# Attention after three LoRA layers on one Trainium2 core: factors stored by head and group, the second normalisation between the root's steps, and other places for the next weights

## The chip, the cores and the metric

The kernel runs on one core of a Trainium2 chip. The time is the device time of one execution in microseconds (us). The engines are called PE (the matmul engine), DVE (VectorE), ACT (ScalarE), POOL (GpSimd) and SP (the queue that issues most loads). PEld is PE's loading of the stationary operand, which runs beside the matmul before it.

## The reference

Four residual layers: a gated MLP with low-rank additions, two linear layers with low-rank additions, and attention over a paged cache. The change touches only the attention:

```
x = x + L3(x)          # x: 8 samples x 128 tokens x 512
q = rope(rmsnorm(x Wq^T)); k = rope(rmsnorm(x Wk^T)); v = x Wv^T    # 32 query heads, 8 key heads, D = 128
k_all = [cached keys (512), k]; v_all = [cached values (512), v]      # 640 keys per sample
scores = q k_all^T / sqrt(D);  cached keys past the length masked with -1e30
probs = softmax(scores);  o = probs v_all;  L3 = o Wo^T
```

## The kernel before

The first 290 us are the three low-rank layers. Then follows the attention in 32 units: 4 pairs of key heads (`NPAIR`), and for each pair the 8 samples. A unit has 8 query heads in two groups of 4 (`G` = 2, `REP` = 4). Every product runs in three passes of split operands (high x high, high x low, low x high), so each operand has a high part (a rounding copy, made by ACT) and a low part (the difference, made by DVE, or by POOL for weights, cached keys and values).

The program is written as turns. Each engine has its own function `turn`, and the order within it is the order of its queue; nothing is reordered by a scheduler. A turn does the front of unit n (projections, norms, rotation, scores, masks, exponentials) and the back of unit n-1 (transposes of the probabilities, sums over values, normalisation, output multiplication), interleaved by hand. There are 33 turns: the first has a front only, the last a back only, and 31 have both.

PE in a turn with both halves: transposes of the first group's probabilities, projection of the second four query heads, values of group 0 and of group 1 (`sums`, L1432), the output multiplication of the first four heads (12 matmuls, L1512), four transposes of rotated queries (L1416), six output matmuls, two transposes of rotated keys, six output matmuls, four transposes of the second queries, then eight scores of six matmuls (L1462) with the next unit's 24 projection matmuls (L1395) between them. Both sets of query transposes use `bank1`, and the second must wait until ACT has made the high part (`high`, L1575) and DVE the low part (`low`, L1746) of the first. The first query transposes wait for `s_rope`, which DVE raises after it has multiplied the new keys by the root.

DVE: copy of the queries, the reciprocal of the softmax denominators (`shares`, L1765), low parts of group 0's probabilities (L1732, L1738), the rotation of the first four queries and the keys (L1721 to L1727), low parts of group 1, the normalisation of group 0 (`normalise`, L1773), the reciprocal square root of the norms by three Newton steps of three small instructions each (`root_end`, L1710 to L1712), two scales from it (L1714, L1715), the keys multiplied by the root (L1808), the normalisation of group 1, the rotation of the second four queries with the low part of group 1's values (L1777) inside it, the low parts for the scores, the mask of the cached keys (L1760), and a mask with maximum for each head (L1753, L1756).

The normalisation multiplies values that lie as [feature, query] by 1/denominator, which DVE has as [query, head]. ACT therefore stores the 128 x 8 reciprocals to DRAM (L1607, after `s_rden`) and loads them back spread over all 128 partitions (L1618, after the store's semaphore `s_den`). DMA issues stand in ACT's queue like its other instructions: what is written behind an issue that waits is not begun.

Weights of the next pair come in 20 chunks of 256 KB: SP loads them into a ring, ACT makes the high part (`high_weights`, L1555), POOL the low part (`low_weights`, L1218). Chunks 0 to 11 are made in the last sample's turn (`extra == "next"`, three times), at places given by the table `EARLY` and by `late`; chunks 12 to 19 in the turn after it (`"out"`). POOL's low parts in a "next" turn begin after the first rotation and after the room for the output is free; chunks 4 and 5 wait for the second rotation (`s_rope`).

## Time and profile before

| | us |
|---|---|
| median of 3 runs | 1467.98 (1465.78 to 1471.86) |
| the profiled execution | 1468.85 |
| its span | 1467.2 |
| PE busy | 1381.8 (94%) |
| DVE busy | 1051.9 (72%) |
| ACT busy | 804.4 (55%) |
| POOL busy | 449.0 (31%) |
| chain that ended last: PE, DVE, issue, ACT, DMA | 70%, 13%, 7%, 6%, 3% |
| DVE's reciprocals of two middle turns start at | 612.71 and 648.26 |
| the same around a turn with next weights | 537.89 and 577.29 |

The page says for each engine how long it was busy, and which chain of work ended last. The share of time by engine is an average over the first 290 us and the attention; the turn-by-turn rows below are of one turn in the middle of the second pair, which repeats with little change, and of one "next" turn. In a row of the timeline the bracket tells how long the engine was idle before it and what ended that.

### The profile page before, as it was taken

How to read it: one execution, taken by the hardware profiler on the slowest of the kernel's cores; microseconds unless marked ns; L12 is line 12 of the kernel's file. 1: busy time of each engine (PE TensorE's matmuls, PEld its weight loads, DVE VectorE, ACT ScalarE, POOL GpSimd, SP SyncE). 2: the span in 40 equal slices, each digit the busy share in tenths (PEclk: the TensorE clock that was granted, in tenths of full speed). 3: DMA queues.
4: the chain of work that ended last, by engine and by line, in shares of the span. 5: the costliest groups of instructions: out<-in, count | busy, mean ns of one | idle time of the engine just before them, and what ended most of it. 6: DMA issues, size and time to landing. Idle time of an engine off the chain costs nothing.

```text
span 1467.2 us, 26375 instructions
## 1 busy us (share of the span) xinstructions
PE 1381.8 (94%) x7308; PEld 1157.6 (79%) x7308; DVE 1051.9 (72%) x2569; ACT 804.4 (55%) x1888; POOL 449.0 (31%) x483
## 2 busy tenths in 40 slices
PE   5999999989999999999999999999998999999996
PEld 5888888878888887888888778877887888888884
DVE  4532447778777787777777777777777777777774
ACT  5532334375555556655555666555556665555553
POOL 4000000562222236522222455222224552222321
PEclk9999999999999999999999999999999999999998
DMA  8111303553333344333232452332225522222211
GB/s 307 45 58 44 108 18 117 198 181 75 81 80 78 74 124 143 90 77 73 72 72 72 136 149 74 73 72 72 72 73 148 138 73 72 75 76 72 72 37 29
DMA packets 149049, 135.59 MB, mean 92 GB/s; under 512 B 95360, under 2 KB 114176, under 8 KB 148736
## 3 DMA queue, kind: packets, MB, share of 16 engines
q1 hardware_dynamic: 127328, 83.35, 20.4%
q0 software_dynamic: 11728, 34.09, 8.2%
q10 hardware_dynamic: 9936, 17.45, 4.4%
q8 instruction: 29, 0.48, 0.1%
q14 instruction: 28, 0.23, 0.0%
HBM read 117.89 MB, written 16.91 MB: 92 GB/s over the span
## 4 chain that ended last, share of the span: by engine, by line
PE 70%; DVE 13%; issue 7%; ACT 6%; DMA 3%; POOL 0%; SPq 0%; DVEq 0%; ACTq 0%; POOLq 0%
PE bank L1395 16%; PE wide L1462 14%; PE tail L1512 7%; PE wide L1427 7%; PE tail L1432 6%; DVE tail L1773 5%; PE wide L423 4%; PE wide L491 3%; ACT oT L1583 3%; ACT prT L1579 2%; DVE oT L1777 2%; PE tail L423 2%; PE bank L423 2%; PE wide L550 2%; DMA spread<-one_over_denominators 2%
## 5 line engine op out<-in xcount | busy, mean ns | idle before, releaser
L1587 ACT ACTIVATE pr<-pr,nm,q_scale 128x640 f32<-128x640 f32 x256 | 236.4, 923 | 91.0 <-DVE nm L1756 89.1
L1753 DVE CUSTOM_DVE_ANT_0 pr<-wide,bias 128x640 f32<-128x640 f32 x256 | 210.0, 820 | 84.9 <-issue 84.8
L1432 PE MATMUL tail<-prT,vt 128*128 128x512 f32 x960 | 262.7, 408 | 4.6 <-DVE prT L1738 2.4
L1512 PE MATMUL tail<-woT,oT 128*128 128x512 f32 x768 | 205.3, 412 | 42.0 <-DVE oT L1777 42.0
L1201 POOL TENSOR_TENSOR tick<-tick 128x1 f32<-128x1 f32 x127 | 26.2, 206 | 614.1 <-PE wide L1462 524.4
L1432 PEld LDWEIGHTS tail<-prT,vt 128*128 128x128 f32 x960 | 168.0, 188 | 54.7 <-DVE prT L1738 17.0
L1512 PEld LDWEIGHTS tail<-woT,oT 128*128 128x128 f32 x768 | 140.2, 192 | 84.6 <-DVE oT L1777 49.4
L1732 DVE TENSOR_TENSOR prT<-wide,prT 128x1024 fp32r<-128x1024 f32 x128 | 153.8, 1222 | 62.0 <-ACT prT L1579 61.8
L1462 PE MATMUL wide<-kT,qT 128*128 128x320 f32 x512 | 161.7, 316 | 0.5 <-DVE mx L1753 0.5
L1462 PE MATMUL wide<-kT_low,qT 128*128 128x320 f32 x512 | 158.7, 310 | 0.0
L1462 PE MATMUL wide<-kT,oT 128*128 128x320 f32 x512 | 158.4, 309 | 0.0
L1579 ACT CAST prT<-wide 128x1024 fp32r<-128x1024 f32 x128 | 126.8, 1016 | 53.3 <-PE wide L1427 52.0
L1583 ACT CAST oT<-tail 128x512 fp32r<-128x512 f32 x64 | 37.5, 587 | 194.5 <-DVE tail L1773 194.5
L1427 PEld LDWEIGHTS wide<-ident,pr 128*128 128x128 f32 x1024 | 115.4, 141 | 20.0 <-issue 9.0
L1427 PE MATMUL wide<-ident,pr 128*128 128x128 f32 x1024 | 128.8, 274 | 0.9 <-DVE mx L1753 0.9
L1395 PE MATMUL bank<-wkvT,xTb 128*128 128x512 f32 x372 | 111.5, 394 | 0.0
L1395 PE MATMUL bank<-wq0T,xTb 128*128 128x512 f32 x372 | 106.2, 393 | 0.0
L1462 PEld LDWEIGHTS wide<-kT,qT 128*128 128x128 f32 x512 | 96.7, 189 | 10.7 <-DVE mx L1753 1.0
L1462 PEld LDWEIGHTS wide<-kT_low,qT 128*128 128x128 f32 x512 | 96.7, 189 | 8.9
L1462 PEld LDWEIGHTS wide<-kT,oT 128*128 128x128 f32 x512 | 96.6, 189 | 0.0
L1240 POOL TENSOR_TENSOR vt<-v_raw,vt 128x1280 fp32r<-128x1280 f32 x32 | 95.1, 2973 | 2.6
L1395 PE MATMUL bank<-wq1T,xTb 128*128 128x512 f32 x372 | 92.9, 398 | 0.0
(236 smaller groups left out, 2555.8 us busy)
## 6 DMA issues: line engine op xcount, KB each, us to landing
w_ring<-pair_weights SPq DMA_DIRECT2D x80, 256.0 KB, 4.2
k_raw<-k_pages SPq DMA_DIRECT2D x512, 32.0 KB, 2.8
v_raw<-v_pages SPq DMA_DIRECT2D x512, 32.0 KB, 1.7
spread<-one_over_denominators ACTq DMA_DIRECT2D x32, 512.0 KB, 4.5
xTb<-x_transposed POOLq DMA_DIRECT2D x31, 512.0 KB, 4.8
out<-y POOLq DMA_DIRECT2D x32, 256.0 KB, 6.0
rope<-rope_tables SPq DMA_DIRECT2D x31, 256.0 KB, 2.6
w_raw<-w_gate_up SPq DMA_DIRECT2D x10, 512.0 KB, 3.3
```

The costliest lines, as they stand in the source:

```text
L423: last = nc.tensor.matmul(gate_up_place(j, c, w), wT[:, j % 2, w, w_part, k, :], x_half(x_part, k, c), start=(k == 0 and w_part + x_part = ...
L1240: nc.gpsimd.tensor_tensor(vt[1][:, :, :], v_raw[:, :, :], vt[0][:, :, :], ALU.subtract).then_inc(s_vs, 1)
L1395: last = nc.tensor.matmul(bank[i][:, :], x[:, x_part, k, :], w[:, w_part, k, :], start=(step == 0), stop=(step == NPROD - 1))
L1427: last = nc.tensor.transpose(wide[w][:, c * P:(c + 1) * P], piece, ident[:, :])
L1432: last = nc.tensor.matmul(tail[g][:, :], vt[v_part][:, j, g * D:(g + 1) * D], prT[p_part][:, j, :], start=(j == 0 and v_part + p_part == 0 ...
L1462: last = nc.tensor.matmul(out, (qT, qT_low)[q_part][:, g, i * S:(i + 1) * S], (kT, kT_low)[k_part][:, g, c * (NK // 2):(c + 1) * (NK // 2) ...
L1512: last = nc.tensor.matmul(tail[0][:, :], oT[:, o_part, h // REP, (h % REP) * S:(h % REP + 1) * S], woT[w_part][:, h, :], start=(h == 0 and ...
L1579: ac.copy(prT[0][:, 2 * w:2 * w + 2, :], wide[w][:, :].rearrange("p (j c) -> p j c", j=2)).then_inc(s_phi, 1)
L1583: ac.copy(oT[:, 0, g, :], tail[g][:, :]).then_inc(s_ohi, 1)
L1587: ac.activation(pr[h][:, :], pr[h][:, :], ACT.Exp, bias=nm[:, h:h + 1], scale=q_scale[:, 0, head(h)], accum_out=den[:, h:h + 1]).then_inc( ...
L1732: v.tensor_tensor(prT[1][:, 2 * w:2 * w + 2, :], wide[w][:, :].rearrange("p (j c) -> p j c", j=2), prT[0][:, 2 * w:2 * w + 2, :], ALU.subt ...
L1753: v.tensor_tensor_reduce(halves(pr[h][:, :]), scores, halves(bias[:, :]), 1.0, -3.0e38, ALU.add, ALU.max, mx[:, h:h + 1]).then_inc(s_sfree, 1)
```

## The change

- The scratch in DRAM for the reciprocals is laid out by group, head and query, where it was by query and head. Each group has its own store and its own spread, with semaphores of their own. The store's runs are single elements; the spread tile is read contiguously by `normalise`, where it was read with a step of 8 elements.
- Group 0's reciprocals are computed at the end of the turn before, ahead of the last mask; its store is the first thing of ACT's back half. The spreads stand behind the first and behind the second squares.
- DVE: the Newton steps are apart, with the second normalisation between the first and the second step and the low part of group 1's values between the second and the third. The two scales stand behind the second rotation. In a "next" turn the root begins behind the low values of group 0.
- PE: the first query transposes wait for the first rotation (`s_step`), no longer for the keys' multiplication; the key transposes wait for that.
- The high parts of the next weights: chunk 0 before the copy of the second queries, chunk 1 before group 1's first high part, chunks 2 and 3 before its second, 4 and 5 behind the values, 6, 7 and 8 between the high parts of queries and keys, 9 to 11 among the exponentials.

The diff, with unchanged stretches cut:

```diff
--- before.py
+++ after.py
...
     rope_scratch = nc.dram_tensor("rope_tables", [B, P, 4 * D], F32).ap()
-    share_scratch = nc.dram_tensor("one_over_denominators", [P * HP], F32).ap()
+    share_scratch = nc.dram_tensor("one_over_denominators", [G, REP * S], F32).ap()
...
     pr = [place(135168 + h * 2560 if h < 6 else 163840 + (h - 6) * 2560, f"pr{h}", [P, NK]) for h in range(HP)]
-    spread = place(135168, "spread", [P, P, HP])
+    spread = place(135168, "spread", [P, G, REP * S])
     k_raw = place(155648, "k_raw", [P, NPP, G, PSIZE])
...
     s_rden = sem("denominator_ready")
-    s_den = sem("one_over_denominators_stored")
-    s_spread = sem("one_over_denominators_spread")
+    s_den = [sem(f"one_over_denominators_stored{g}") for g in range(G)]
+    s_spread = [sem(f"one_over_denominators_spread{g}") for g in range(G)]
     s_norm = sem("values_normalised")
...
     NSTEP = 16
+    TURNED = 2
     TURN = [FRONT[i] + BACK[i] for i in range(2)]
...
-    EARLY = {"next": ((0,), (1,), (2, 3), (4, 5, 6, 7), (8,), (9,), (10,)), "out": ((), (), (), (), (12, 13), (14,), (15,)), None: ((),) * 7}
+    EARLY = {"next": ((0,), (1,), (2, 3), (4, 5), (6,), (7,), (8,)), "out": ((), (), (), (), (12, 13), (14,), (15,)), None: ((),) * 7}
...
         if extra == "next":
-            return [11] if h == 3 else []
+            return [h + 7] if 2 <= h < 5 else []
         return [h + 14] if extra == "out" and 2 <= h < 6 else []
...
-        TURNED, MASKED = 2, NSTEP
+        MASKED = NSTEP
...
-                pe.wait_ge(s_rope, n * G + 1 + FIRST)
+                pe.wait_ge(s_step, n * NSTEP + TURNED)
                 transposes(1, [ra[:, i, :] for i in range(REP)])
...
             if front:
+                pe.wait_ge(s_rope, n * G + 1 + FIRST)
                 transposes(0, [ra[:, REP + i, :] for i in range(G)])
...
+            def early(place):
+                for i in EARLY[extra][place]:
+                    if i == 0:
+                        act.wait_ge(c_full[0], before[0] + 1)
+                        act.wait_ge(c_full[1], before[1] + 1)
+                    high_weights(chunk_pair(pair, extra), i)
+            def store_shares(g):
+                act.wait_ge(s_rden, u * G + g + 1)
+                act.dma_start(share_scratch[g].rearrange("(i p) -> p i", p=P), rden[:, g * REP:(g + 1) * REP],
+                              allow_slow_non_contiguous=True).then_inc(s_den[g], 16)
+            def spread_shares(g):
+                act.wait_ge(s_den[g], u * 16 + 16)
+                act.dma_start(spread[:, g, :], share_scratch[g:g + 1].to_broadcast([P, REP * S])).then_inc(s_spread[g], 16)
...
             if back:
+                store_shares(0)
                 high_probs(0, 0)
-                act.wait_ge(s_rden, u + 1)
-                act.dma_start(share_scratch.rearrange("(p h) -> p h", h=HP), rden[:, :]).then_inc(s_den, 16)
+                store_shares(1)
                 high_probs(0, 1)
...
             if back:
-                act.wait_ge(s_den, u * 16 + 16)
-                act.dma_start(spread[:, :, :].rearrange("p q h -> p (q h)"),
-                              share_scratch.rearrange("(o n) -> o n", o=1).to_broadcast([P, P * HP])).then_inc(s_spread, 16)
+                spread_shares(0)
             if front:
+                early(0)
                 arrive()
...
                     act.wait_ge(s_xs[0], 16 * BLK)
-            def early(place):
-                for i in EARLY[extra][place]:
-                    if i == 0:
-                        act.wait_ge(c_full[0], before[0] + 1)
-                        act.wait_ge(c_full[1], before[1] + 1)
-                    high_weights(chunk_pair(pair, extra), i)
             if back:
-                early(0)
+                spread_shares(1)
+                early(1)
                 high_probs(1, 0)
-                early(1)
+                early(2)
                 high_probs(1, 1)
...
                 copy_values(0)
-            early(2)
             own = BACK[0] if back else 0
...
-            def root_end():
+            def newton():
                 x_, y_, t_ = var[:, :], rs[:, :], nt[:, :]
-                for _ in range(3):
-                    then(v.tensor_tensor(t_, y_, y_, ALU.mult))
-                    then(v.scalar_tensor_tensor(t_, t_, -0.5, x_, ALU.mult, ALU.mult))
-                    then(v.scalar_tensor_tensor(y_, t_, 1.5, y_, ALU.add, ALU.mult))
+                then(v.tensor_tensor(t_, y_, y_, ALU.mult))
+                then(v.scalar_tensor_tensor(t_, t_, -0.5, x_, ALU.mult, ALU.mult))
+                then(v.scalar_tensor_tensor(y_, t_, 1.5, y_, ALU.add, ALU.mult))
+            def scales():
                 v.tensor_scalar(q_scale[:, 0, :], rs[:, :], SCALE, None, ALU.mult)
...
-            def rotate(h0, m0, kinds, between=None):
+            def rotate(h0, m0, kinds):
                 for k0, m, kind in kinds:
...
                     v.tensor_tensor(o, q, cos_w.to_broadcast([P, m, D]), ALU.mult)
-                    if between:
-                        between()
                     v.tensor_tensor(s[:, :, 0:half], q[:, :, half:D], sin_w[:, :, 0:half].to_broadcast([P, m, half]), ALU.mult)
...
-            def shares():
-                dve.wait_ge(s_exp, u * HP + HP)
-                v.reciprocal(rden[:, :], den[:, :]).then_inc(s_rden, 1)
+            def shares(of, g):
+                dve.wait_ge(s_exp, of * HP + (g + 1) * REP)
+                v.reciprocal(rden[:, g * REP:(g + 1) * REP], den[:, g * REP:(g + 1) * REP]).then_inc(s_rden, 1)
...
                 dve.wait_ge(s_pv, u * G + g + 1 + FIRST)
-                if g == 0:
-                    dve.wait_ge(s_spread, u * 16 + 16)
-                summed = tail[g][:, :].rearrange("p (i q) -> p i q", i=REP)
-                v.tensor_tensor(summed, summed, spread[:, :, g * REP:(g + 1) * REP].rearrange("p q i -> p i q"), ALU.mult).then_inc(s_norm, 1)
+                dve.wait_ge(s_spread[g], u * 16 + 16)
+                v.tensor_tensor(tail[g][:, :], tail[g][:, :], spread[:, g, :], ALU.mult).then_inc(s_norm, 1)
...
             if back:
-                shares()
+                shares(u, 1)
                 low_probs(0, 0)
...
                 low_probs(1, 0)
-            if front:
+            if front and extra != "next":
                 root_begin()
...
             if front:
-                root_end()
+                if extra == "next":
+                    root_begin()
+                newton()
+            if back:
+                normalise(1)
+            if front:
+                newton()
+            if back:
+                low_values(1)
+            if front:
+                newton()
                 keys = ra[:, REP:REP + G, :]
                 v.tensor_tensor(keys, keys, rs[:, REP:REP + G].rearrange("p (h o) -> p h o", o=1).to_broadcast([P, G, D]), ALU.mult).then_inc(s_rope, 1)
-            if back:
-                normalise(1)
-                if not front:
-                    low_values(1)
-            if front:
-                rotate(REP + G, REP, ((REP + G, REP, 0),), (lambda: low_values(1)) if back else None).then_inc(s_rope, 1)
+                rotate(REP + G, REP, ((REP + G, REP, 0),)).then_inc(s_rope, 1)
+                scales()
...
                     mask_max(h)
+                    if h == HP - 2:
+                        shares(n, 0)
                 assert at.n == NSTEP, at.n
```

What this moves, from the instructions as they stand in the program. First DVE in the last sample's turn of the first pair, before, from the third Newton step on (`nt`, `rs`: its steps; `q_scale`: the scales; `tail<-tail,spread`: the normalisation; `oT<-tail,oT`: the low part of the values):

```order
L1710 TENSOR_TENSOR nt<-rs 128x10
L1711 SCALAR_TENSOR_TENSOR nt<-nt,var 128x10
L1712 SCALAR_TENSOR_TENSOR rs<-nt,rs 128x10
L1714 TENSOR_SCALAR q_scale<-rs 128x10
L1715 TENSOR_SCALAR q_scale<-rs 128x10
L1808 TENSOR_TENSOR ra<-ra,rs 128x256
L1773 TENSOR_TENSOR tail<-tail,spread 128x512
L1721 TENSOR_TENSOR ra<-qk,rope 128x512
L1777 TENSOR_TENSOR oT<-tail,oT 128x512
L1724 TENSOR_TENSOR rb<-qk,rope 128x4x64
L1725 TENSOR_TENSOR rb<-qk,rope 128x4x64
```

and now, from the second normalisation on:

```order
L1781 TENSOR_TENSOR tail<-tail,spread 128x512
L1721 TENSOR_TENSOR nt<-rs 128x10
L1722 SCALAR_TENSOR_TENSOR nt<-nt,var 128x10
L1723 SCALAR_TENSOR_TENSOR rs<-nt,rs 128x10
L1785 TENSOR_TENSOR oT<-tail,oT 128x512
L1721 TENSOR_TENSOR nt<-rs 128x10
L1722 SCALAR_TENSOR_TENSOR nt<-nt,var 128x10
L1723 SCALAR_TENSOR_TENSOR rs<-nt,rs 128x10
L1826 TENSOR_TENSOR ra<-ra,rs 128x256
L1733 TENSOR_TENSOR ra<-qk,rope 128x512
L1734 TENSOR_TENSOR rb<-qk,rope 128x4x64
L1735 TENSOR_TENSOR rb<-qk,rope 128x4x64
```

The normalisation of group 1 stood behind all steps, the scales and the keys' multiplication (`ra<-ra,rs`). Now two of the three Newton steps and the keys stand behind it, and the scales further down.

Then ACT in the same turn, before, from the spread's issue to the high part of the queries (`wkvT`, `wq0T`: chunks of the next weights; `prT`: high parts of the probabilities, one instruction for half a group, the last for its new keys):

```order
L1618 DMA spread<-one_over_denominators 128x1024
L1622 COPY qk<-bank 128x512
L1569 ACTIVATE bank,ss<-bank 128x128 x4
L1555 CAST wkvT<-w_ring 128x512
L1579 CAST prT<-wide 128x1024
L1555 CAST wkvT<-w_ring 128x512
L1579 CAST prT<-wide 128x1024
L1642 CAST prT<-bank 128x512
L1583 CAST oT<-tail 128x512
L1555 CAST wkvT<-w_ring 128x512 x2
L1583 CAST oT<-tail 128x512
L1555 CAST wq0T<-w_ring 128x512 x4
L1575 CAST qT<-bank 128x512
```

and now:

```order
L1608 DMA spread<-one_over_denominators 128x512
L1557 CAST wkvT<-w_ring 128x512
L1641 COPY qk<-bank 128x512
L1571 ACTIVATE bank,ss<-bank 128x128 x4
L1608 DMA spread<-one_over_denominators 128x512
L1557 CAST wkvT<-w_ring 128x512
L1581 CAST prT<-wide 128x1024
L1557 CAST wkvT<-w_ring 128x512 x2
L1581 CAST prT<-wide 128x1024
L1655 CAST prT<-bank 128x512
L1585 CAST oT<-tail 128x512 x2
L1557 CAST wq0T<-w_ring 128x512 x2
L1577 CAST qT<-bank 128x512
```

Before the high part of the queries (`qT`) stood four chunks behind the second copy of values (`oT`); now two. Chunks 0, 2 and 3 stand earlier.

## Rows read from the trace of the kernel before

**Rows 1.** Waits, whole span: engine line <- releaser: us in total, times, longest
```profile
PEld tail L1512 <- DVE oT L1777: 49.4, 31, 1.9
```

**Rows 2.** Timeline, weight loads, middle turn: start us, us, what, xcount [idle before <-releaser]
```profile
659.17 1.22 PEld L1432 LDWEIGHTS tail<-prT,vt 128*128 128x128 f32 x6 [0.26 <-DVE prT L1732]
...
660.87 0.53 PEld L1432 LDWEIGHTS tail<-prT,vt 128*128 128x128 f32 x3 [0.48 <-DVE prT L1738]
...
661.68 2.61 PEld L1512 LDWEIGHTS tail<-woT,oT 128*128 128x128 f32 x12 [0.29 <-issue]
...
666.45 1.23 PEld L1512 LDWEIGHTS tail<-woT,oT 128*128 128x128 f32 x6 [1.53 <-DVE oT L1777]
...
669.33 0.59 PEld L1416 LDWEIGHTS bank<-ident,ra 128*128 128x128 f32 x4
```

**Rows 3.** Timeline, DVE, the same turn
```profile
659.03 1.19 DVE L1773 TENSOR_TENSOR tail<-tail,spread 128x512 f32<-128x512 f32 x1
...
660.13 0.68 DVE L1738 TENSOR_TENSOR prT<-bank,prT 128x512 fp32r<-128x512 f32 x1
...
660.87 0.69 DVE L1777 TENSOR_TENSOR oT<-tail,oT 128x512 fp32r<-128x512 f32 x1
...
661.48 0.16 DVE L1710 TENSOR_TENSOR nt<-rs 128x10 f32<-128x10 f32 x1
...
663.31 0.17 DVE L1714 TENSOR_SCALAR q_scale<-rs 128x10 f32<-128x10 f32 x1
...
663.59 0.42 DVE L1808 TENSOR_TENSOR ra<-ra,rs 128x256 f32<-128x256 f32 x1
...
663.93 1.12 DVE L1773 TENSOR_TENSOR tail<-tail,spread 128x512 f32<-128x512 f32 x1
...
665.71 0.69 DVE L1777 TENSOR_TENSOR oT<-tail,oT 128x512 fp32r<-128x512 f32 x1
```

**Rows 4.** Timeline, DVE, the first turn, second rotation to the low part
```profile
305.69 0.68 DVE L1721 TENSOR_TENSOR ra<-qk,rope 128x512 f32<-128x512 f32 x1
...
307.69 0.68 DVE L1746 TENSOR_TENSOR oT<-bank,qT 128x512 fp32r<-128x512 f32 x1
```

**Rows 5.** Timeline, ACT and its queue, the middle turn
```profile
648.50 0.33 ACTq L1607 DMA_DIRECT2D one_over_denominators<-rden  x1
...
654.59 1.01 ACT L1579 CAST prT<-wide 128x1024 fp32r<-128x1024 f32 x1 [0.41 <-PE wide L1427]
```

**Rows 6.** DMA issues: out<-in, queue, xcount, KB each, us to landing
```profile
spread<-one_over_denominators ACTq DMA_DIRECT2D x32, 512.0 KB, 4.5
...
one_over_denominators<-rden ACTq DMA_DIRECT2D x32, 4.0 KB, 1.4
...
seqlens<-itok_B SPq DMA_DIRECT2D x1, 4.0 KB, 3.5
...
bias<-L_cond_bias SPq DMA_DIRECT2D x1, 2.0 KB, 4.0
```

**Rows 7.** Timeline, POOL, DVE, PE and ACT, the first turn with next weights
```profile
546.43 2.53 POOL L1218 TENSOR_TENSOR wkvT<-w_ring,wkvT 128x512 fp32r<-128x512 f32 x2
...
546.51 1.23 DVE L1705 TENSOR_SCALAR rs<-var 128x10 int32<-128x10 int32 x1
...
551.53 1.27 DVE L1710 TENSOR_TENSOR nt<-rs 128x10 f32<-128x10 f32 x1
...
556.29 0.66 PE L1416 MATMUL bank<-ident,ra 128*128 128x128 f32 x4 [1.52 <-DVE ra L1808]
...
558.63 2.93 PE L1512 MATMUL tail<-woT,oT 128*128 128x512 f32 x6 [1.68 <-DVE oT L1777]
...
561.59 1.63 PE L1512 MATMUL tail<-woT,oT 128*128 128x512 f32 x6
...
557.75 2.18 ACT L1555 CAST wq0T<-w_ring 128x512 fp32r<-128x512 f32 x4
```

**Rows 8.** Windows, same turn: us, busy (x instructions) by engine, PEclk, DMA share, GB/s
```profile
559.00:562.00 3.00, 3.00 (x10) 2.27 (x10) 1.62 (x3) 2.06 (x5) 1.88 (x2) 0.58 0.25 56
```

## The prediction, made before the changed kernel was run

> **What bounds the kernel now.** I read the chain that ended last first: the matmul engine, PE, holds most of it and DVE comes next. Then the waits: the longest stall of PE that comes back regularly is in front of the output multiplication, 31 times, 49.4 us in total, and always behind the same DVE line [rows 1]. Then one middle turn (a "turn" is one sample of one pair of key heads, about 35.5 us long, 32 of them), engine by engine. On PE's weight loads the reader should see four holes after the scores of the turn are read: 0.26, 0.48, 0.29 and 1.53 us [rows 2]; almost everywhere else the loads are back to back, so a middle turn has about 2.6 us to win and little more. DVE's rows [rows 3] tell why the 1.53 exists: between 661.48 and 663.59 DVE does the whole root (nine small steps and two scales), then multiplies the new keys, and only at 663.93 normalises the second group, 1.12 us long, though PE had delivered it by then. ScalarE's copy and DVE's low part follow, and PE continues at 666.45.
>
> **Second normalisation between the root's steps, and contiguous factors.** The first normalisation starts at 659.03 and the next DVE row stands 1.10 later; the low-part row of equal size (128x512 from PSUM against an SBUF tile) takes 0.68 to 0.69 [rows 3]. The old factors are read with a step of 32 bytes, the new ones contiguously. The trace has no contiguous multiplication that writes PSUM, so I bound it: 1.19 (nothing gained) to 0.69. I take 0.69, the row that differs only in where the result goes.
> Then, in the same turn's clock: first normalisation 659.03 to 659.72; low part of the new keys' probabilities starts at 659.63 instead of 660.13 and is done at 660.31. PE's loads of the block before it end at 659.17 + 1.22 = 660.39, so the 0.48 hole closes. The first group's low part starts 0.50 earlier too, at 660.37, and PE starts the output multiplication at 661.18 instead of 661.68. First root step 660.98 to 661.60 (three ops at 0.205: 661.48 to 663.31 is nine of them). Second normalisation 661.60 to 662.29; PE's last three sums, begun at 660.39, are through by then. The second group's low part followed the start of its normalisation by 1.78 (663.93 to 665.71, with ScalarE's copy between them), now by 1.78 - 0.43 = 1.35: 662.95 to 663.64, and the second root step (0.6) fits in beside the copy. PE's twelve output matmuls take 2.61 [rows 2], to 663.79, and the four query transposes 0.59, to 664.4: the second group is ready 0.7 us before PE asks for it. The 1.53 goes.
>
> **Transposes of queries not held for keys.** They now wait for the rotation, which is over long before. In a middle turn this is worth nothing by itself (PE came at 661.68 + 2.61 = 664.3, the keys were multiplied from 663.59 on), but it is needed: the keys' multiplication moves back to about 664.2 (third root step from 663.56). The two key transposes follow six output matmuls (1.23), at 665.7, when the keys have been ready since 664.6. Nothing lost.
>
> **What is late next.** PE reaches the last four transposes 2.88 after it resumed the output multiplication, as before (666.45 to 669.33 [rows 2]): 664.5 + 2.9 = 667.4. They overwrite the bank whose low part DVE must have read. DVE: rotation from 664.52 (the keys' multiplication takes 0.34 to the next start); with nothing inside it, it takes 2.00 from its first op to the low part (305.69 to 307.69 [rows 4]), plus 0.28 for the two scales, now behind it (663.31 to 663.59 [rows 3]), so the low part starts at 666.80 and ends at 667.48. PE goes on at 667.52. **A middle turn gains 669.33 - 667.52 = 1.81 us.** From there on the order is that of before (eight scores with 24 projection matmuls, PE without holes). The one reciprocal put before the last mask costs 0.2 on DVE, inside the pause that DVE has before each mask, since PE's scores set the pace there. If I am wrong on the contiguous reading, both normalisations are 0.5 longer: the 0.48 hole stays, the DVE chain ends 0.94 later, and the turn gains 0.87.
>
> **Factors by head and group.** Before, one store of 128 runs of 32 bytes, issued at 648.50 [rows 5], landing after 1.4, then one spread of 512 KB, 4.5 [rows 6]. Now two stores, each of 512 runs of 4 bytes, and two spreads of half the size. The first store's factors are computed in the turn before, so it goes out by 648 or earlier. No row shows such a store. The nearest is the bias load, 512 elements of 4 bytes one by one: 4.0 us against 3.5 for its neighbour with 128 runs of 32 bytes [rows 6], so 0.5 for 384 more runs. Bounds for the store: 1.4 (runs are free) to 5.6 (all of the 1.4 grows with the runs, times 4); I take 1.9, by the bias row. Then both stores land by 651; the first spread goes out at about 650.5, the second behind the second squares, by 654.6 at the latest; with the old 4.5 they land at 655.0 and 659.1, and the normalisations ask at 659.0 and 661.6. Covered. The wait to look at is not DVE's but ScalarE's: its issue of the second spread waits for the second store, and the high part of the second group's probabilities (654.59 [rows 5]) is queued behind it; PE waits for that at once. The cover is 654.59 - 648.50, less 0.3 for issuing the spread: about 5.8 us from the store's issue.
> The Trainium skill, DMA: Bandwidth & Descriptors, Rules for kernel authors, speaks against this edit: a non-contiguous last dimension becomes one descriptor per element, and one should rearrange. The bias row agrees that it costs something, 0.5 us, but not that it matters here; should each descriptor cost its full share, the sum is that of the third rival.
>
> **Other places for the next weights.** Three turns carry the next pair's weights. In the one at 538 to 577, PE waits 1.52 before the query transposes and 1.68 before the output multiplication, and the six matmuls after that take 2.93 where the next six take 1.63 [rows 7]; the granted clock is 0.58 over 559 to 562 [rows 8], so after these two waits PE was for a while at the lower of its two levels. Two things made it late: DVE's small root steps stretched from 0.17 to 1.2 when GpSimd was subtracting weights (1.23 at 546.51, beside GpSimd's two from 546.43 to 548.96; 1.27 at 551.53), and ScalarE had four weight chunks (2.18) ahead of the queries' high part. After: chunks 2 and 3 go before the second high part, where ScalarE waits for PE; GpSimd's four subtractions, 1.27 each from 546.43, end near 551.5, and the root begins near 551.0 (0.5 ahead of 551.53), so about 0.5 of collision is left. Gain: 1.52 + 1.68 + 1.30 = 4.5, and the 0.5 further up cancels the collision's. **4.5 us in each of three turns.** Bounds: 1.8 (as a middle turn) to 6.
>
> **The sum**, against the profiled execution (1468.85 us; the median of the runs shown is 1467.98, 0.9 less). 31 turns have both halves: 28 x 1.81 = 50.7; 3 x 4.5 = 13.5; the last half turn 0.5 by the shorter first normalisation; the first turn nothing, since its low part still gates it. Together 64.7: 1404.2, and 1403.3 against the median. I say 1404.
>
> **The rivals.**
> *A: the strided read was not the cost.* The multiplications stay at 1.15, since both results go to PSUM, which no other DVE row shows. For it: that absence. Against: 0.46 more than each row of equal size. 28 x 0.87 + 3 x 3.5 = 35: 1433.
> *B: the weight turns gain no more than the others*, because the second rotation's signal, which lets GpSimd start the next subtractions, now stands ahead of the two scales; or because the store, with 4 times the runs, meets the weight loads in the queues. For it: a root step held for 1.23 beside GpSimd. Against: each scale takes 0.17 and stands right behind the signal, so both may have begun before GpSimd does. 31 x 1.81 + 0.5 = 57, less 1.3 in six turns = 49: 1419.
> By the Trainium skill, SBUF — State Buffer, Who interferes with whom, a DVE op in its two-port mode and a GpSimd op exclude each other for the whole instruction; the stretched root steps agree with that.
> *C, on the other side: the 4-byte store holds ScalarE.* If a store takes 5.6 and the second queues behind the first, it lands near 648 + 11.2 = 659, ScalarE's high part comes some 4.5 late, and each turn loses 4.5 - 1.8 = 2.7: 31 x 2.7 = 84, 1552. It decides from about 5.8 us after the issue; the gain is eaten at 5.8 + 1.8 = 7.6. Against it: the bias row, and that 1.4 is mostly the same for any size.
>
> **How the numbers follow.** Forecast 0.67, A 0.12, B 0.13, C 0.08, of which 0.06 slower, 0.01 no change. A measurement of this kernel can tell about 0.5% (7 us). So faster 0.93, same 0.01, slower 0.06. The range: below, if all holes but 0.26 and 0.29 close and the weight turns give 6: 28 x 2.0 + 18 + 0.5 = 75, 1393; above it takes in A, 1436. What is left out is C and a little more.
>
> **What would show it.** The hole of 1.53 before the output multiplication gone; DVE's two normalisations at about 0.69; a wait of 0.1 to 0.2 before the last four transposes, released by DVE's low part of the queries; turn period 33.7 between two reciprocals of the same group; weight turns under 36; ScalarE's second spread issued near 653, without holding the high part behind it; store landing near 2. Wrong if the normalisations stay at 1.15, or the second spread goes out after the high part's place.

## The result, and the profile after

The changed kernel takes 1625.8 us (median), the kernel before 1467.4: ratio 1.106 (95% interval 1.102 to 1.111), 158 us slower. One of its four runs took 1838.4 at a granted clock of 0.726; the ratio is of the other three (1621.3 to 1627.6). I had said 1404, with a range of 1393 to 1436. The profiled execution took 1624.0 (span 1622.4) at a mean granted clock of 0.939, where before it was 0.989.

The chain that ended last, of the page of the changed kernel (shares by engine, then by line):

```profile
PE 36%; DMA 24%; issue 19%; ACT 10%; DVE 9%; ACTq 1%; DVEq 0%; POOL 0%; POOLq 0%
DMA one_over_denominators<-rden 19%; PE tail L1513 8%; PE tail L1433 8%; DMA spread<-one_over_denominators 5%; PE wide L423 3%; PE wide L491 3%; ACT pr L1589 2%; ACT bank L1571 2%; PE bank L1417 2%; PE bank L423 2%; PE tail L423 2%; PE wide L550 2%; DVE prT L1742 2%; ACT prT L1581 1%; DVE nm L1766 1%
```

A transfer of 2 KB, the store of the factors, is now the largest single item. The waits of the changed kernel, from the whole list (engine line <- releaser: us in total, times, longest):

```profile
DVE prT L1742 <- ACT prT L1581: 224.9, 67, 16.6
...
ACT qk L1641 <- DMA one_over_denominators<-rden: 147.2, 26, 7.4
...
PEld tail L1433 <- DVE prT L1742: 88.4, 39, 10.4
```

The wait of [rows 1] is gone from the list; ScalarE's wait for the store stands there with three times its size. One middle turn of the changed kernel, ScalarE and its queue (it answers to [rows 5]):

```profile
691.87 0.38 ACTq L1602 DMA_DIRECT2D one_over_denominators<-rden  x1
...
692.68 0.38 ACTq L1602 DMA_DIRECT2D one_over_denominators<-rden  x1
...
701.64 0.34 ACTq L1608 DMA_DIRECT2D spread<-one_over_denominators  x1
702.09 0.58 ACT L1641 COPY qk<-bank 128x512 f32<-128x512 f32 x1 [6.07 <-issue]
...
704.06 0.34 ACTq L1608 DMA_DIRECT2D spread<-one_over_denominators  x1
704.44 1.93 ACT L1581 CAST prT<-wide 128x1024 fp32r<-128x1024 f32 x2 [0.52 <-DMA one_over_denominators<-rden]
```

The first spread leaves 9.8 us after the first store was issued, because it waits for the store; ScalarE's copy of the queries (6.07 idle) and the high parts of the second group's probabilities stand behind it: these begin 12.0 us after the second reciprocal, where in [rows 5] they began 6.3 after it. PE's weight loads in the same turn (it answers to [rows 2]):

```profile
703.97 0.42 PEld L1417 LDWEIGHTS bank<-ident,pr 128*128 128x128 f32 x4 [2.68 <-ACT bank L1571]
706.77 5.44 PEld L1433 LDWEIGHTS tail<-prT,vt 128*128 128x128 f32 x15 [2.37 <-DVE prT L1742]
712.25 2.71 PEld L1513 LDWEIGHTS tail<-woT,oT 128*128 128x128 f32 x12
...
715.56 1.24 PEld L1513 LDWEIGHTS tail<-woT,oT 128*128 128x128 f32 x6
...
718.77 0.42 PEld L1417 LDWEIGHTS bank<-ident,ra 128*128 128x128 f32 x4 [0.37 <-DVE oT L1756]
```

The reader sees three things. There are two new holes (stretches in which PE waits), of 2.68 and 2.37 us. Behind them 15 sums' loads take 5.44, 0.36 each, where nine take 1.92 in the second run below, 0.21 each: the granted clock is 0.58 over 706.8 to 712.3, where these sums run, and 1.00 over the 7.7 us behind them, so after the holes PE ran for a while at the lower of its two levels (1.2 instead of 2.4 GHz). Over the whole turn the clock is 0.91. And the hole of 1.53 before the output multiplication's second part is closed. DVE, the same turn (it answers to [rows 3]):

```profile
708.26 0.69 DVE L1781 TENSOR_TENSOR tail<-tail,spread 128x512 f32<-128x512 f32 x1
...
712.68 0.70 DVE L1781 TENSOR_TENSOR tail<-tail,spread 128x512 f32<-128x512 f32 x1 [1.89 <-PE tail L1433]
```

Both normalisations have the forecast length. DMA issues of the changed kernel (us to landing last; the store's own is not shown):

```profile
w_ring<-pair_weights SPq DMA_DIRECT2D x80, 256.0 KB, 7.1
...
spread<-one_over_denominators ACTq DMA_DIRECT2D x64, 256.0 KB, 6.9
...
out<-y POOLq DMA_DIRECT2D x32, 256.0 KB, 10.9
```

Before, the weights' ring landed in 4.2 and the output's store in 6.0: transfers that have nothing to do with the store became slower too. A half-sized spread takes longer than the whole one did (6.9 against 4.5).

Where the 155 us of span are: between the reciprocals of the second group (31 intervals) the three weight turns take 49.5, 50.5 and 51.3 where they took 39.4, 40.2 and 41.1 (30.6 in all), the 28 others 39.66 on average where they took 35.43 (118.4). Some 6 come behind the last.

### The profile page after: what moved, and what is told of

It reads as the page before. It is cut to its first block, busy times and chain, and to the rows that moved or that the text cites. A ratio compares the mean times of both kernels' runs of the same rounds, so it can differ in the third digit from the quotient of the medians.

```text
span 1622.4 us, 26595 instructions
## 1 busy us (share of the span) xinstructions
PE 1436.4 (89%) x7308; PEld 1196.8 (74%) x7308; DVE 1015.6 (63%) x2601; ACT 797.7 (49%) x1888; POOL 448.1 (28%) x483
## 3 DMA queue, kind: packets, MB, share of 16 engines
q0 software_dynamic: 11728, 34.09, 15.1%
## 4 chain that ended last, share of the span: by engine, by line
PE 36%; DMA 24%; issue 19%; ACT 10%; DVE 9%; ACTq 1%; DVEq 0%; POOL 0%; POOLq 0%
DMA one_over_denominators<-rden 19%; PE tail L1513 8%; PE tail L1433 8%; DMA spread<-one_over_denominators 5%; PE wide L423 3%; PE wide L491 3%; ACT pr L1589 2%; ACT bank L1571 2%; PE bank L1417 2%; PE bank L423 2%; PE tail L423 2%; PE wide L550 2%; DVE prT L1742 2%; ACT prT L1581 1%; DVE nm L1766 1%
## 5 line engine op out<-in xcount | busy, mean ns | idle before, releaser
L1433 PE MATMUL tail<-prT,vt 128*128 128x512 f32 x960 | 307.2, 469 | 85.1 <-DVE prT L1742 78.4
L1433 PEld LDWEIGHTS tail<-prT,vt 128*128 128x128 f32 x960 | 211.8, 231 | 144.0 <-DVE prT L1742 88.4
L1513 PE MATMUL tail<-woT,oT 128*128 128x512 f32 x768 | 197.0, 400 | 0.0
L1581 ACT CAST prT<-wide 128x1024 fp32r<-128x1024 f32 x128 | 123.2, 1013 | 12.5 <-DMA one_over_denominators<-rden 10.4
L1641 ACT COPY qk<-bank 128x512 f32<-128x512 f32 x32 | 18.7, 585 | 159.1 <-DMA one_over_denominators<-rden 147.2
```

Source lines behind the costliest of these rows:

```text
L1433: last = nc.tensor.matmul(tail[g][:, :], vt[v_part][:, j, g * D:(g + 1) * D], prT[p_part][:, j, :], start=(j == 0 and v_part + p_part == 0 ...
L1513: last = nc.tensor.matmul(tail[0][:, :], oT[:, o_part, h // REP, (h % REP) * S:(h % REP + 1) * S], woT[w_part][:, h, :], start=(h == 0 and ...
L1581: ac.copy(prT[0][:, 2 * w:2 * w + 2, :], wide[w][:, :].rearrange("p (j c) -> p j c", j=2)).then_inc(s_phi, 1)
```

## The experiments

The question is first which of the edits costs so much. Theory 1: the element-wise store lands after 9 to 10 us and holds ScalarE's queue. Rival: the split transfers or the new order cost. In the diffs below, access patterns are written in short. "Landing" is the time from a transfer's issue to its end, as the list of DMA issues has it (median). Where that list has none for a store, I take the time from its issue to the issue of the spread that waits for it, for the first group's store and as a median over the turns. With a store that lands early this measure still gives some 2.4 us (second run), since the spread's place in the queue comes only then.

**First run: stores in rows, read with a step.**

```diff
-  share_scratch[g].rearrange("(i p) -> p i", p=P)      # 512 runs of 4 bytes
+  share_scratch[g].rearrange("(p i) -> p i", i=REP)    # 128 runs of 16 bytes
-  v.tensor_tensor(tail, tail, spread[:, g, :])
+  v.tensor_tensor(tail as "p i q", ..., spread[:, g, :] as "p (q i) -> p i q")
```

> The changed kernel with one thing undone: each group's factors are stored as 128 runs of 16 bytes (token, head), and the normalisation reads the spread factors with a step of 16 bytes. The two stores, the two spreads and the whole order stay. Theory 1 (the store written element by element lands after 9 to 10 us instead of 1.4 and holds ScalarE's queue): the store lands in about 2 us, ScalarE's copy after the squares is no longer held, the wait of it on the store (147 us in 26 waits) goes, and the time falls from 1626 to about 1404 if a step of 16 bytes reads as fast as contiguous data, to about 1430 if it reads like the step of 32 bytes (1.15 to 1.19 us per normalisation instead of 0.70). Theory 2 (two small spreads and two stores instead of one of each are the cost, or the new order of DVE and the weights): the time stays above 1550, since nothing of that is changed.

Measured: 1436.7, ratio to before 0.979 (0.975 to 0.983). The store is the whole loss.

**Second run: the same stores, contiguous read.**

> As the first run, with the stores of 128 runs of 16 bytes, but the normalisation reads contiguously, as in the changed kernel. What is left out is the right pairing of factors with values; every instruction, size and wait of the changed kernel is there except the store's access pattern. Theory 1 (the element-wise store alone is what went wrong with the forecast): 1404, with a range of 1393 to 1420, turns of 33.7 and normalisations of 0.70. Theory 2 (split transfers or order): above 1550. The difference to the first run is the price of reading the spread with a step of 16 bytes: nothing, or up to 28 turns of 0.94 = 26 us.

Measured: 1413.8, ratio 0.963 (0.960 to 0.967). The store lands in 1.7 us (median of all 64; 1.5 for the first group's, 2.3 for the second's, which follows it in the queue). PE's loads in a middle turn of it, which is the turn that I had worked out:

```profile
678.29 1.92 PEld L1433 LDWEIGHTS tail<-prT,vt 128*128 128x128 f32 x9 [0.28 <-DVE prT L1741]
680.30 2.65 PEld L1513 LDWEIGHTS tail<-woT,oT 128*128 128x128 f32 x12
682.99 0.59 PEld L1417 LDWEIGHTS bank<-ident,ra 128*128 128x128 f32 x4
683.55 1.23 PEld L1513 LDWEIGHTS tail<-woT,oT 128*128 128x128 f32 x6
...
686.95 0.42 PEld L1417 LDWEIGHTS bank<-ident,ra 128*128 128x128 f32 x4 [0.56 <-DVE oT L1755]
```

And DVE:

```profile
678.15 0.69 DVE L1780 TENSOR_TENSOR tail<-tail,spread 128x512 f32<-128x512 f32 x1
...
680.86 0.70 DVE L1780 TENSOR_TENSOR tail<-tail,spread 128x512 f32<-128x512 f32 x1 [0.19 <-DVE rs L1722]
...
682.28 0.69 DVE L1784 TENSOR_TENSOR oT<-tail,oT 128x512 fp32r<-128x512 f32 x1 [0.25 <-ACT oT L1585]
...
685.83 0.17 DVE L1725 TENSOR_SCALAR q_scale<-rs 128x10 f32<-128x10 f32 x1
...
686.20 0.69 DVE L1755 TENSOR_TENSOR oT<-bank,qT 128x512 fp32r<-128x512 f32 x1
```

Of the holes only 0.28 and 0.56 are left. Middle turns take 34.07 (before 35.54), the weight turns 35.6, 35.4 and 35.6 (before 39.4, 40.2 and 41.1).

**Third run: the layout alone, in the kernel before.**

> The kernel before with the layout alone changed: one store of 1024 runs of 4 bytes (by head, then token), one spread of 512 KB, a contiguous read by the normalisation. Order of work, places of weights, root and transposes as before. Theory 1: the store lands after about 10 us (8 to 18, if it grows with the number of runs), ScalarE stands in front of the copy of the second projections till about 648.5 + 10 = 658.5 or later instead of 652, and each of 31 turns loses 4 to 8 us less the 1.0 that the two normalisations get shorter: 1560 to 1690. Theory 2 (the layout is harmless, the splitting or the order did it): 1440 to 1470, a little faster than before by the shorter normalisations.

Measured: 1668.3, ratio 1.136 (1.132 to 1.141). ScalarE in one turn of it:

```profile
707.75 0.38 ACTq L1607 DMA_DIRECT2D one_over_denominators<-rden  x1
...
718.47 0.35 ACTq L1618 DMA_DIRECT2D spread<-one_over_denominators  x1
718.93 0.59 ACT L1622 COPY qk<-bank 128x512 f32<-128x512 f32 x1 [7.80 <-DMA one_over_denominators<-rden]
```

One edit of the four explains the sign. 1024 runs take 11.1 us to the spread (median of 32 turns), 512 take 9.2: hardly a price per run.

**Fourth run: the order alone.**

> The changed kernel with the factors' path of before: one store of 128 runs of 32 bytes, one spread of 512 KB, a normalisation that reads with a step of 32 bytes. New are only the order of DVE (second normalisation between the root's steps), the transposes of queries that do not wait for the keys, and the places of the next weights. Theory 1 with my working for the middle turn without contiguous factors (0.87 per turn, 28 turns, and 3.5 in each of three weight turns): 1433. Theory 2 (the new order costs): above 1468, most of it in the weight turns. If the places of the weights are worth no more than a middle turn: 1440.

Measured: 1440.3, ratio 0.981 (0.977 to 0.985), middle turns 34.94: 0.60 gained where I had 0.87. The weight turns take 36.4, 35.9 and 37.3, 3.7 less than before where I had 3.5. The order and the places together gain without the new layout; which of the two does it in the weight turns, this run cannot tell.

Next, what makes the store slow. All four have the second run as base, and one store more per group.

```diff
   act.dma_start(share_scratch[g] ..., rden[:, g * REP:(g + 1) * REP])   # rows of 16 bytes
+  act.dma_start(spare_scratch[g] ..., ...)                             # the store in question, into memory that nobody reads
```

> Base is the second run (stores of 128 runs of 16 bytes, contiguous normalisation, 1413.8; the right pairing of factors with values is left out in this and the next three kernels). Behind each store the same factors are stored once more, element by element (512 runs of 4 bytes, neighbours in memory from different partitions), into a place that nobody reads; ScalarE waits for that store only before it copies the normalised values, some 11 us after the issue. Theory 1 (the slow store costs by holding ScalarE's queue in front of the next copy): 1414 to 1430, with two more issues of 0.4 us on ScalarE. Theory 2 (the element-wise writes slow the other transfers, whatever waits for them: GpSimd's queue had 15.1% of the DMA engines' time in the changed kernel against 8.2% before): above 1450, with the spread landing after 7 us instead of 4.5 and the output's store after 11 instead of 5.6.

Measured: 1570.3, ratio 1.068 (1.065 to 1.071). The signs of theory 2 are there: the spread lands after 7.3, the output's store after 11.7, and GpSimd's queue has 15.4% of the DMA engines' time. But ScalarE is held all the same, in a way that theory 1 did not have. ScalarE in one turn:

```profile
672.51 0.41 ACTq L1605 DMA_DIRECT2D one_over_denominators<-rden  x1
...
672.95 0.46 ACTq L1606 DMA_DIRECT2D spare<-rden  x1
...
673.92 0.34 ACTq L1611 DMA_DIRECT2D spread<-one_over_denominators  x1
...
681.36 0.33 ACTq L1611 DMA_DIRECT2D spread<-one_over_denominators  x1
681.72 1.93 ACT L1583 CAST prT<-wide 128x1024 fp32r<-128x1024 f32 x2 [3.74 <-DMA one_over_denominators<-rden]
```

The second cheap store, behind the first slow one in the same queue, let its spread go only 8.9 us after its own issue (9.2 on the median), though in the second run this store lands after 1.8 in the same turn and 2.3 on the median. Not waiting for a slow store didn't help what was queued behind it. How much of the changed kernel's loss comes by this hold and how much by the slower transfers, no run separates.

> As the run before, but the elements of the additional store lie 64 bytes apart in memory, and the spread waits for it as well as for the cheap store. If the number of writes sets the landing, it is about 9 us as in the changed kernel, and the time near 1626 to 1650. If writes of neighbouring elements by different partitions block each other, the landing falls to 2 to 3 us and the time is 1414 to 1430.

Measured: 1418.8, ratio 0.965 (0.960 to 0.969); landing 3.5 us, with the same 512 writes of 4 bytes. Neither their number nor their width is slow by itself. The output's store lands after 5.2 and GpSimd's queue has 9.5%, so the other transfers are not slowed either.

> The additional store has 256 runs of 8 bytes, neighbours from different partitions, and is waited for. 128 runs of 16 bytes land in 1.8 us, 512 of 4 bytes in 9.3 (median of 32 first stores), 1024 in 11.1. If the number of runs sets it in a straight line between the first two, 4.3 us: then ScalarE waits some 2 us per turn and the time is 1460 to 1500. If it is the small element that is slow (any element-wise write pays some 7 us), 8 to 9 and near 1600; if runs of 8 bytes already go like those of 16, 2 to 3 and 1414 to 1430.

Measured: 1424.3, ratio 0.968 (0.965 to 0.972), landing 4.1.

> The additional store has 128 runs of 4 bytes (one head of the group), neighbours from different partitions, and is waited for. By a straight line through 512 runs at 9.3 and 1024 at 11.1 it would take 8.0 us and the time be near 1600: a fixed price of some 7.5 us of any store with 4-byte elements. If the number of runs sets it, 1.8 to 2.5 us and 1414 to 1425.

Measured: 1586.5, ratio 1.079 (1.074 to 1.083). 128 elements, 512 bytes in all, do most of the harm (173 of the 212 us between the second run and the changed kernel). The wait for this store takes 8.3 us on the median, and 8.0 in this turn:

```profile
722.35 0.45 ACTq L1605 DMA_DIRECT2D spare<-rden  x1
...
730.34 0.33 ACTq L1611 DMA_DIRECT2D spread<-one_over_denominators  x1
730.78 0.59 ACT L1644 COPY qk<-bank 128x512 f32<-128x512 f32 x1 [4.35 <-DMA spare<-rden]
```

**Two ways to keep the contiguous read.**

```diff
-  matmul(tail[g], vt, prT[:, j, :])                        # e9: moving operand by head, token
+  matmul(tail[g] as "p q i", vt, prT[:, j, :] as "p (i q) -> p q i")
-  oT[:, o_part, g, head's 128 columns]                     # e9: weights of the output multiplication
+  (oT[:, o_part, g, :] as "p (q i) -> p i q")[:, head, :]
```

> The factors stay in rows of 16 bytes (token, head), as in the first run, and the rest follows them: PE reads the probabilities in the order token, head when it sums the values (a step of 512 bytes in the moving operand), so that the sums in PSUM, the factors and the normalised values all have that order and the normalisation is contiguous on both sides; PE loads the values' weights for the output multiplication with a step of 16 bytes. Nothing is left out. If PE reads and loads with a step as fast as without (0.25 us per sum in the stretch, 0.21 per load), the time is that of the second run, 1414. If the moving read gets slower, each of the 30 sums per turn pays: 10% more is 30 x 0.02 = 0.6 per turn, about 1435; twice the time is 7 per turn and about 1630.

Measured: 1450.8, ratio 0.989 (0.987 to 0.992). Of this kernel's page:

```profile
L1433 PE MATMUL tail<-prT,vt 128*128 128x512 f32 x960 | 298.7, 454 | 3.1 <-DVE prT L1741 3.1
...
L1513 PEld LDWEIGHTS tail<-woT,oT 128*128 128x128 f32 x768 | 189.4, 311 | 4.0 <-DVE oT L1784 1.1
```

The second run has 404 and 188 there. A turn got 1.20 longer (35.27), which comes to 0.04 for each of the 30 sums with a step of 512 bytes in the moving operand, if they are the whole of it. The loads with a step take 311 instead of 188 ns, but lie beside the matmuls.

```diff
-  share_scratch[g].rearrange("(i p) -> p i", p=P)            # e12: after the changed kernel
+  share_scratch[g].rearrange("(j p k) -> p j k", p=P, k=2)   # 256 runs of 8 bytes
+  spread read as "p (j q k) -> p j k q"                      # a step of 8 bytes
```

> The changed kernel with the store in 256 runs of 8 bytes (pair of heads, token, head of the pair), and a normalisation that reads the factors with a step of 8 bytes. Nothing is left out. The store should land in about 3.5 us, as the additional one of 8-byte runs (4.1 behind another). A step of 16 bytes cost 1.06 us per normalisation, one of 32 bytes 1.17, none 0.69. If the price goes by the bytes that are skipped (4 times too many at 16), a step of 8 bytes gives 0.75 to 0.85 and 1420 to 1425; if any step costs the same, 1.06 and 1437.

Measured: 1419.9, ratio 0.968 (0.965 to 0.970), and a step of 8 bytes costs nothing. The normalisation in this kernel (the second run, with no step, has 694 ns), then in the first run:

```profile
L1782 DVE TENSOR_TENSOR tail<-tail,spread 128x512 f32<-128x512 f32 x64 | 44.5, 695 | 6.7 <-DVE rs L1723 4.6 <-DMA spread<-one_over_denominators 1.5 <-PE tail L1433 0.5
```

```profile
L1781 DVE TENSOR_TENSOR tail<-tail,spread 128x512 f32<-128x512 f32 x64 | 67.9, 1061 | 5.1 <-DVE rs L1722 4.6 <-PE tail L1433 0.3
```

**What about the arrangement is slow.**

```diff
   spare_scratch[g] as "(a x) -> a x", a=16, [:, 0:8]     # e10: 8 elements, then a gap up to 128 bytes
   spare_scratch[g] as "(r a k) -> a r k", a=16, k=2      # e11: 8-byte runs, groups of partitions mixed
   spare_scratch[g] as "(a x) -> a x", x=32, [0:8, 0:16]  # e13: 16 elements in aligned 64 bytes
   spare_scratch[g] as "(a x) -> a x", x=32, [0:8, 8:24]  # e14: the same, 32 bytes further
```

> As the run with 128 additional elements of 4 bytes (store landed after some 8.4 us, 1586), but every 8 neighbours stand in a block of their own, 128 bytes from the next: still 4-byte writes next to each other, but 64 bytes of memory now take them from 8 partitions instead of 16. Theory L (what blocks are writes of different groups of partitions, as different DMA engines carry them, into the same 64 bytes): the landing falls to 2 to 3 us and the time to 1414 to 1425. Theory W (4-byte writes next to each other are slow as such, two in one word of 8 bytes): 8 us and about 1586, as before. The additional store is waited for; the right pairing of factors with values is left out here and in the next kernel, as in the second run.

Measured: 1410.8 (one run, like the next three), landing 2.7 us. Theory W falls: neighbours of 4 bytes in one word of 8 are cheap here.

> The counterpart: an additional store of 128 runs of 8 bytes, laid so that every 64 bytes of memory take runs of partitions that are 8 apart (the order in memory is row within the group, then group). Theory L: every 64 bytes are written by 8 groups of partitions, and the store is slow, 8 us or more, 1586 or above. Theory W: whole words of 8 bytes are never shared, so 2 to 3 us and 1414 to 1425.

Measured: 1415.8, landing 3.7. Theory L falls as well, at least for runs of 8 bytes.

> 128 additional elements of 4 bytes, waited for, as in the runs with 128 elements side by side (landing some 8.4 us, 1586) and in blocks of 8 (2.7 us, 1411). Here 16 neighbours stand side by side in 64 aligned bytes, and the next block begins 128 bytes on. Theory N (slow is what puts 16 separate writes into the same 64 bytes; 8 and fewer are cheap, which also fits the two runs with 8-byte runs): 8 us and about 1586. Theory R (slow is a long unbroken run of written memory, 512 bytes there, 64 here): 2 to 4 us and 1411 to 1425. The right pairing of factors with values is left out here and in the next kernel, as in the second run.

Measured: 1443.8, with middle turns of 34.08 and the loss in and behind the weight turns (40.5, 40.8 and 35.8 in a row). The wait for the store takes 3.5 us on the median of the first group's. The same measure gives 8.3 with 128 elements side by side, 3.4 with 256 runs of 8 bytes, 2.7 with blocks of 8.

> The same 8 blocks of 16 elements, each shifted by 32 bytes, so that it lies half in one and half in the next 64 aligned bytes: 8 writes in each. Theory N with 64 aligned bytes: 2.7 to 4 us and 1411 to 1425. If this one is slow and the one before as well, the number of side-by-side writes counts and not the aligned 64 bytes (or the block that counts is 128 bytes long); if both are cheap, theory R stands.

Measured: 1440.1, the same picture, and again 3.5. The two don't differ, so theory N falls. The landing is what theory R gave, but both times lie above its 1411 to 1425, and far below 1586. Part of that may be the chip: both ran on the one where the stores of 8 bytes land later as well, and where their weight turns are as long (the run with the old places of the weights, below); but there the turn behind the first of them takes 34.0, here 40.8 and 39.0.

**The last 0.33 us of a middle turn.**

```diff
-  scales()                 # behind the second rotation
   low(1, ...)
   low(2, ...)
   mask_keys()
+  scales()
```

> The kernel with pairs of heads (stores of 8-byte runs, 1419.9, right result) with one edit: DVE computes the two scales of the scores not before the low part of the queries but behind the mask of the keys, where it waits 0.64 us for ScalarE in any case. PE waits 0.56 us before its last four transposes, for exactly that low part. Theory 1 (DVE's chain after the rotation sets this wait): the low part starts 0.37 us earlier, the wait falls from 0.56 to about 0.2, and 31 turns gain 0.3 to 0.37 each: 1408 to 1411. Theory 2 (ScalarE's high part or PE's own order comes late right behind it): less than 0.1 per turn, 1417 to 1420.

Measured: middle turns 33.70 instead of 34.07, as theory 1 said:

```profile
657.47 0.42 PEld L1417 LDWEIGHTS bank<-ident,ra 128*128 128x128 f32 x4 [0.24 <-DVE oT L1756]
```

The whole took 1423.2, ratio 0.969 (0.967 to 0.971), not the 1408 to 1411 of theory 1: the weight turns (41.7, 38.7, 39.9) and those behind them gave the gain back. This was another chip than that of the 1419.9, and the stores of 8 bytes landed after 4.4 on it instead of 3.7.

> The same kernel with pairs of heads with one edit undone: the next weights stand in the places of before, and in the three weight turns the root begins before the second low part of probabilities again. My forecast gave these turns 4.5 us each, of which 1.48 is what a middle turn got; the rest of some 3 was put down to the new places. Theory 1: the three weight turns get 3 us longer each and the time is 1429. Theory 2 (the gain came with the freed DVE and ScalarE, whatever the places): 1420, no difference. Middle turns stay at 34.07 either way.

Measured: 1428.7, ratio 0.973 (0.971 to 0.976). That is theory 1's number, but not its reason: the weight turns take 40.7, 41.1 and 38.5, no longer than those of the run before. That run shared its chip and has 28 x 0.37 = 10 us less in its middle turns, yet is only 5.5 faster. So with 8-byte stores the new places are worth nothing that I can show, and may cost; with cheaper stores they weren't tried alone.

**The two candidates side by side.**

```diff
-  spread_shares(1)         # e18, on top of the later scales
   early(1)
   high_probs(1, 0)
+  spread_shares(1)
```

In e18 the first weight chunk also moves behind the second squares.

> The kernel with pairs of heads, unchanged, beside the next one on the same chip. It gave 1419.9 (ratio 0.968) on one chip. If the chips differ in how fast small stores land (3.7 us there, 4.4 us where the version with later scales ran), it is 1420 on a chip like the first and 1430 to 1434 on one like the second; the middle turns stay at 34.07 on both, and the three weight turns (38.4 on average before) take the difference.

Measured: 1419.8, ratio 0.969 (0.967 to 0.970), on another chip than before (1419.9 there); the stores land after 4.0.

> The version with later scales (33.70 per middle turn, 1423.2), with two moves on ScalarE: the wait for the second store and the second spread stand behind the first high part of the second group's probabilities, and the first weight chunk behind the second squares. In the weight turns ScalarE had waited 3.3 us for the weights' ring in front of the queries' copy and 2.7 for the second store. Theory 1: these waits hold the chain, the three weight turns fall from 40.1 to 36 or less, and the time to 1409 to 1412, 10 us or more below the kernel beside it. Theory 2: the second spread now comes late for the second normalisation, which asks 13.5 us after the second reciprocal; issued some 7.3 us after it and landing in 5.8 it has 0.4 to spare, and if the landing is slower each turn pays up to 1 us: 1430 to 1450.

Measured: 1415.8, ratio 0.965 (0.964 to 0.967), 4 us below the kernel beside it. Middle turns 33.70, which would be 10 us; the weight turns stay at 39.6, 40.3 and 38.2 (beside 38.6, 39.8 and 38.3), so the waits that I moved did not hold them, and theory 1 is wrong on them. The loss of theory 2 did not come. This is the fastest version that leaves nothing out: 50 us under before, 210 under the changed kernel.

## Why the prediction was wrong

The forecast named the right wait and the wrong size. By its steps:

- **Factors by head and group: this step failed.** I took 1.9 us for the store, bounded it by 5.6, and had cover for 5.8. It takes 9.2 (median of the first group's, issue to the spread that waits for it), and 8.3 even with 128 elements; so the cover of 5.8 is gone in each turn. The bound was not one: it scaled a row of 32-byte runs with the count. The row I went by, the bias [rows 6], is a read of single elements and not a write, and it has no neighbours written at the same time. By the Trainium skill, DMA: Bandwidth & Descriptors, Rules for kernel authors, every element becomes its own descriptor; the runs say that 512 such writes cost 3.5 us when they lie apart, so this is not yet the harm.
- **Rival C** (0.08) had the mechanism: the store holds ScalarE. It gave 2.7 us per turn and 1552. The middle turns lost 4.2 on average and the weight turns 10. What it lacked: the store is longer than its bound, the wait for the first store already holds ScalarE (I put it on the second), the other transfers get slower as well (DVE waited 21.4 us in all for spreads, before 2.0), and PE sums at the lower clock behind its new holes.
- **Contiguous factors: right.** 0.69, and worth 23 us against a step of 16 bytes (first against second run). Rival A, that the step was not the cost, is refuted. The price by the step of the read: none 0.69, 8 bytes 0.695, 16 bytes 1.06, 32 bytes 1.15 (before) and 1.17 (fourth run). The Trainium skill, SBUF — State Buffer, Door 1: The DMA port swizzle, tells of lines of 16 bytes that want at least two hits each. The runs agree with two hits (8 bytes), but not with its remark that 4 fp32 elements of step are free: at 16 bytes the op was half longer.
- **The middle turn: right but for one term.** In the second run's turn (19.10 us later by its reciprocals) the first normalisation, its low part and the output multiplication start within 0.02 of my times. From there DVE slips: 0.16 before the second normalisation, 0.23 at the second low part, 0.19 at the keys and 0.30 at the queries' low part, so that PE waits 0.56 and not 0.1 to 0.2. I had put ops back to back whose inputs come from the op or engine before (the marked 0.19 and 0.25), and counted 0.28 for scales that take 0.37. Gain 1.47 instead of 1.81: over 28 turns 9.5 us, about the distance from 1404 to 1413.8.
- **Queries not held for the keys; 0.48 and 1.53 close:** right, as the loads of the second run show.
- **The weight turns:** 4.5 each forecast, 4.7 measured in the second run (120.7 for the three, now 106.6). Rival B (no more than in others) is refuted for that run. In the changed kernel its second reason, that the store meets the weight loads, did appear: ScalarE waited 22.0 us in three waits for the weights' ring (2.8 in the second run). That the new places bring the gain is not shown. Nor do [rows 7] show that it is DVE's two-port mode that stretches the root steps: one of the two, at 551.53, multiplies a tensor by a tensor and is stretched as much as the other.

## What to carry to other kernels

Before a store is made element-wise to save an engine a strided read, price the store by a write of that very pattern, and ask who waits for it and what is queued behind it: here 0.94 us of DVE per turn were bought with a store that holds ScalarE's queue for 8 us more. A small step in between can have both, as here: runs of 8 bytes store in 3.7 to 4.4 us, and a read with a step of 8 bytes costs DVE nothing. And an upper bound scaled from a cheap pattern does not bound another pattern.

## What the runs showed of the hardware

- Writes of 4 bytes side by side over 512 bytes or more are a case of their own: 128 of them took 8.3 us to the spread, 512 of them 9.2, 1024 of them 11.1. Cheap were 512 writes 64 bytes apart (3.5), 128 in blocks of 8 (2.7), 256 or 128 runs of 8 bytes in either order (4.1, 3.7), runs of 16 (1.8) and 32 bytes [rows 6]. Blocks of 16 were waited for as long as runs of 8 bytes (3.5 against 3.4), but their kernels lay between (1440 and 1444, one run each). What is left is the unbroken stretch of such writes (64 bytes cheap to wait for, 512 not), and no run varied it alone. The mechanism stays open: the number of writes, their width, shared words of 8 bytes and 16 writes per 64 bytes are each excluded as the sole cause. Not tried is whether single elements of partitions far apart, mixed as the 8-byte runs were, are slow over a short stretch.
- Such a store slows others. In the four kernels with one (the changed one, third, fifth and eighth run) the output's store lands after 10.4 to 11.7 us, in all others after 5.2 to 6.3. GpSimd's queue moves the same 34.09 MB in all of them, in 15.1 to 16.2% of the DMA engines' time against 8.2 to 11.7%. The changed kernel's page says:

```profile
q0 software_dynamic: 11728, 34.09, 15.1%
```

- A slow store holds a cheap one behind it in the same queue (fifth run: 8.9 us instead of 1.8).
